# A second edge sort in four steps per block, one more part of edge sums between the experts, and row products in bf16 thirds

## The chip, the core and the metric

The kernel runs on one core of one Trainium2 chip. The metric is the device time of one launch in microseconds; the kernel before takes 3007.59 us, the median of three runs (3007.4 to 3023.45).

## The reference, cut to what matters

Two layers of a graph network over N = 3125 nodes of width 256. The part that this change touches is the feed-forward block of layer 0: a small graph attention over 65536 edges that yields a gate for each node and expert, and four experts, and beside them the sort of the 50000 edges that layer 1 will need.

```python
h = (x_flat @ W_gat).reshape(M, HEADS, NUM_EXPERTS)          # 4 heads x 4
e = leaky_relu(a_src[src] + a_dst[dst], 0.2)
ee = exp(e - segment_max(e, dst)[dst])
alpha = ee / (segment_sum(ee, dst)[dst] + 1e-16)
agg = segment_sum(h[src] * alpha[:, :, None], dst) + b_gat
scores = layernorm(agg).reshape(M, HEADS, NUM_EXPERTS).mean(1)   # top 2, softmax -> gate g
for ei in range(NUM_EXPERTS):
    hh = gelu(x @ W1[ei] + b1[ei])
    out = out + g[..., None] * (hh @ W2[ei] + b2[ei])
# layer 1: the same kind of edge sum over (src, dst), grouped by src
```

## The kernel before, in words

Nodes lie in NT = 25 tiles of P = 125. Edges sorted by their goal node lie in SBUF as columns of 128: COLS0 = 512 columns for this block, COLS1 = 400 for layer 1. The stage is `gat_edges` (L2297). One Block (from L2330) holds everything that follows, and the order on each engine is written out by hand.

**Slots.** `Experts0` (L2689) works through 52 chunks of two node tiles (the last chunk of each expert has one). Each half of a chunk's work is a slot: `tensor_down` of a tile (4 f32 products of 256 columns), or `tensor_up` for the next chunk (4 f32 products of 250 columns). There are 100 downs and 102 ups, so 202 slots, numbered 0 to 201. On TensorE, VectorE and ScalarE the expert work of a slot is followed by `s1....slot(n)` (the second sort) and `by....slot(n)` (rows by products). Slots 38, 118, 163, 197 and 201 are downs, so the line L2787 (`vector_down`, VectorE's part of a down) marks their time.

**The second sort** is `SortBeside` (L1419), 25 blocks of 16 columns. Slots 6 to 30 count. From `rank_at` = 38 each block has USES = 5 slots: `tensor_again` (16 products) and four `tensor_same` (5 products each) share a ring of two PSUM banks, four of the five slots have a `tensor_rank` (12 products). VectorE has `vector_again` and `vector_turned` (one-hot tables), `vector_within` (a scan), `vector_choose` and `vector_base`. So ranks fill slots 38 to 162. At slot 163 VectorE computes all places (`vector_places`) and the first two tables of the moves; from `move_at` = 168 each of 27 blocks moves in two slots (`tensor_half`: 8 products of 400 columns; `vector_move`: four large comparisons and products; `scalar_half`: 4 Signs). The last 20 of these 54 slots, 202 to 221, have no expert work: they are run after the loop, and then `vector_finish` and `tensor_end`.

**Rows by products.** `RowsByProducts` (L1800) makes the last 64 of the 512 columns of gathered rows. In slots 38 to 117, of every five one turns four one-hot tables (`L1874`) and ScalarE copies them to f32 (`L1890`); in each of the other four TensorE multiplies one of them with the node table `m.hg` (20 of its 24 words, 500 columns of f32, L1882), and VectorE picks a row (`vector_take`: L1844 and L1848). The other 448 columns are gathered by GpSimd (L2378).

**Edge sums.** They are made in four parts of columns, PARTS = 0, 128, 256, 400, 512. Parts 0 and 1 start at slots 86 and 150 (PART_AT) and are spread over eleven slots: scores, maxima, Exp on ScalarE, weigh, then two steps of scans. Parts 2 and 3 are run after the sort has ended.

**The end of the Block.** SyncE has one queue. It stores each chunk's outputs (`ex.store`), then waits for VectorE's mark `all_by` after slot 201, loads X back from DRAM (L2360, 3.2 MB), waits for it, loads expert 1's outputs back (L2365, 3.2 MB), waits for the end of the sort (`pre3`), loads experts 2 and 3 back (6.4 MB) and stores parts 2 and 3 of the sums (`keep`, L2333; 256 columns, 3.1 MB). The next Block, `join_nodes` (L2042), begins when the engines have come through this one; its GpSimd gathers (L2085) and part of its VectorE work wait until all four stores of sums have landed (`r_stored` = 64).

Of the kernel before, what the change touches and what calls it, by code (L numbers as in the profile page):

```python
# [1046 lines left out]
class Sort:  # L1047
# [95 lines left out]
    def vector(self, dve):  # L1143
# [22 lines left out]
        self.vector_finish(dve)  # L1166

# [107 lines left out]
    def vector_finish(self, dve):  # L1275
# [22 lines left out]
        dve.tensor_copy(self.rsum[:, :], ed.key[:, cols - 1:cols]).then_inc(self.row3, 1)  # L1298
        dve.wait_ge(self.pre3, 1)
        dve.tensor_scalar(ed.key[:, :], ed.key[:, :], m.ps[2][:, 0:1], -1.0, ALU.add, ALU.add)  # L1300


    def tensor(self, pe):
# [33 lines left out]
        pe.matmul(m.ps[2][:, 0:1], m.low[:, :], self.rsum[:, :], start=True, stop=True).then_inc(self.pre3, 1)  # L1337
# [81 lines left out]
class SortBeside(Sort):  # L1419
# [3 lines left out]
    USES = 5  # L1423

    def __init__(self, m, ed, key_in, other_in, line_in, sb):
# [41 lines left out]
        self.move_at = self.rank_at + self.USES * self.nb + 5  # L1467
        self.slots = self.move_at + 2 * (self.nm + 2)
# [11 lines left out]
    def block_of(self, n):  # L1480

        return divmod(n - self.rank_at, self.USES)

# [26 lines left out]
    def keys_due(self, n):  # L1510

        t, use = self.block_of(n)
        if n == self.FIRST + self.nb + 1:
            return 2
        return t + 3 if use == 0 and 0 <= t < self.nb - 3 else None
# [90 lines left out]
    def vector_slot(self, dve, n):  # L1606
# [7 lines left out]
        elif a == nb + 1:  # L1614
            self.vector_totals(dve)
            self.vector_again(dve, 1)
        elif a == nb + 3:
            self.vector_starts(dve)
            self.vector_turned(dve, 1)
        elif n == self.rank_at - 2:  # L1620
            self.vector_within(dve, 0)
        elif n >= self.rank_at:
            t, use = self.block_of(n)
            if t < nb:
                if use == 2 and t + 1 < nb:
# [5 lines left out]
                elif use == 4 and t + 2 < nb:  # L1631
                    self.vector_again(dve, t + 2)
                elif use == 0 and 1 <= t < nb - 1:
                    self.vector_turned(dve, t + 1)
            elif n == self.rank_at + self.USES * nb:
# [5 lines left out]
            elif n > self.move_at:  # L1641
# [8 lines left out]
    def tensor_slot(self, pe, n):  # L1650
# [14 lines left out]
        elif n >= self.rank_at:  # L1665
            t, use = self.block_of(n)
            if t < nb:
                if use < 2:
                    self.tensor_same(pe, t, use + 2)
                elif t + 1 < nb:  # L1670
                    if use == 2:
                        self.tensor_again(pe, t + 1)
                    else:
                        self.tensor_same(pe, t + 1, use - 3)
                if use < 4:
                    self.tensor_rank(pe, t, use)
            elif n >= self.move_at:
                self.tensor_half(pe, *divmod(n - self.move_at, 2))

# [76 lines left out]
    def tensor_end(self, pe):  # L1756
        pe.wait_ge(self.row3, 1)
        pe.matmul(self.m.ps[2][:, 0:1], self.m.low[:, :], self.rsum[:, :], start=True, stop=True).then_inc(self.pre3, 1)


    def scalar_slot(self, act, n):
# [9 lines left out]
        elif n >= self.rank_at:  # L1771
            t, use = self.block_of(n)
            if t < nb:
                if use < 2:
                    self.scalar_mask(act, t, use + 2)
                elif use > 2 and t + 1 < nb:
                    self.scalar_mask(act, t + 1, use - 3)
            elif n == self.rank_at + self.USES * nb:
# [21 lines left out]
class RowsByProducts:  # L1800
# [4 lines left out]
    def __init__(self, m, ed, G, W, first, saved, place):  # L1805
# [8 lines left out]
        self.turned = [place(f"gp_turned{i}", [128, self.GROUP * 128]) for i in range(2)]  # L1814
# [2408 lines left out]
```

## Time and profile before

| what | value |
| --- | --- |
| median of the runs | 3007.59 us |
| span of the profiled execution, first to last instruction | 3005.8 us |
| the profiled execution's own time | not given beside its span; the runs are 3007.4 to 3023.45 us |
| the chain that ended last | its first piece starts at 2377.12 us |
| TensorE / VectorE / ScalarE / GpSimd busy over the span | 75% / 61% / 45% / 54% |

A stretch row reads: from:to, length, then for each engine its busy us and number of instructions, the granted TensorE clock (1 is full), the mean busy share of the 16 DMA engines and GB/s. A timeline row reads: start, duration, engine, line, operation, out<-in, shape, count, and in brackets the idle time before it and what ended it.

### The profile page before, as it was taken

The numbers are of one execution on the slowest core, as the hardware profiler recorded it, in microseconds if no ns is written. First come the engines' busy times: TensorE is split into PE (matmuls) and PEld (weight loads), VectorE is DVE, ScalarE is ACT, GpSimd is POOL, SyncE is SP. The second block draws the span as 40 slices with busy tenths as digits, with TensorE's granted clock in tenths as the row PEclk, the third lists the DMA queues.
The fourth block names the chain that finished last, engine by engine and source line by source line (L and its number), as shares of the span: only waits on it lengthen the run. The fifth ranks groups of instructions, "written<-read, shape, count | busy, mean of one in ns | idle before, by whom it ended". The sixth has DMA issues, their size and how long they took to land. (4 is left out here: it accounts for less than half of the span.)

```text
span 3005.8 us, 46144 instructions
## 1 busy us (share of the span) xinstructions
PE 2243.0 (75%) x15376; PEld 1792.1 (60%) x15376; DVE 1843.3 (61%) x4040; ACT 1353.1 (45%) x3268; POOL 1630.6 (54%) x1530
## 2 busy tenths in 40 slices
PE   4487393464599999989622678878774499999998
PEld 4362152453577777877321466666663457999997
DVE  7889556799467887577859566666675830111113
ACT  4368334674312232348706237776672121434343
POOL 0246565466487777778541655777773225344441
PEclk9799696777599999999955788888787599999999
DMA  3240033300333223212542535666662132456335
GB/s 85 65 133 1 19 65 66 68 1 1 63 103 73 63 54 92 65 37 49 135 109 57 128 101 192 209 198 200 206 218 91 37 111 69 139 199 212 127 123 133
DMA packets 186604, 307.78 MB, mean 102 GB/s; under 512 B 90556, under 2 KB 142383, under 8 KB 175698
## 3 DMA queue, kind: packets, MB, share of 16 engines
q1 hardware_dynamic: 109312, 174.45, 19.7%
q0 software_dynamic: 77120, 131.25, 16.1%
q8 instruction: 83, 1.36, 0.2%
q14 instruction: 89, 0.73, 0.1%
HBM read 268.76 MB, written 108.92 MB: 126 GB/s over the span
## 5 line engine op out<-in xcount | busy, mean ns | idle before, releaser
L2378 POOL DMA_INDIRECT ge_near<-gat_src,s_other x448 | 493.3, 1101 | 141.2 <-issue 141.2
L3803 POOL DMA_INDIRECT he_buf<-wh_dram,s_other x400 | 390.3, 976 | 163.1 <-issue 118.5
L983 POOL DMA_INDIRECT pl_table<-s_key,s_other x272 | 305.4, 1123 | 248.7 <-DMA pl_table<-s_key,s_other 172.1
L3298 ACT ACTIVATE x_hT<-bank,x_w 128x128 f32<-128x128 f32 x448 | 164.7, 368 | 262.4 <-PE bank L3240 231.3
L3923 ACT ACTIVATE he_buf<-he_buf,he_e 128x128 f32<-128x128 f32 x800 | 236.4, 386 | 2.5
L3240 PEld LDWEIGHTS bank<-x_xT,x_w 128*128 128x128 f32 x1792 | 208.7, 192 | 2.8
L3240 PE MATMUL bank<-x_xT,x_w 128*128 128x128 f32 x1792 | 208.9, 275 | 0.0
L2769 PE MATMUL bank<-arena 128*125 128x256 f32 x800 | 195.7, 388 | 16.5 <-ACT arena L2777 16.2
L3250 PE MATMUL bank<-x_w,x_hT 128*128 128x256 f32 x896 | 202.5, 379 | 0.0
L4035 DVE SCALAR_TENSOR_TENSOR he_buf<-he_buf,he_cont 128x256 f32<-128x256 f32 x375 | 183.0, 488 | 29.2 <-issue 0.4
L2758 PE MATMUL bank<-XT,arena 128*128 128x250 f32 (+1 forms) x832 | 196.3, 380 | 5.4 <-PEq L73 5.4
L2777 ACT ACTIVATE arena<-bank,arena 128x250 f32<-128x250 f32 (+1 forms) x208 | 84.2, 456 | 247.6 <-PE bank L2758 247.5
L2769 PEld LDWEIGHTS bank<-arena 128*125 128x125 f32 x800 | 146.5, 189 | 55.3 <-ACT arena L2777 22.9
L3250 PEld LDWEIGHTS bank<-x_w,x_hT 128*128 128x128 f32 x896 | 166.0, 190 | 20.3
L2758 PEld LDWEIGHTS bank<-XT,arena 128*128 128x128 f32 x832 | 155.2, 196 | 36.8 <-issue 21.1
L2961 POOL DMA_INDIRECT x_w<-in_L_ffn_fall,x_rows x56 | 55.4, 989 | 151.3 <-DVEq L3044 141.6
L2956 POOL DMA_INDIRECT x_w<-in_L_ffn_rise,x_rows x56 | 56.7, 1012 | 136.5 <-ACT x_hT L3298 85.5
L1796 ACT ACTIVATE arena<-row,arena 128x400 f16<-128x400 f16 x216 | 115.9, 615 | 25.3 <-PE bank L1748 17.7
L3042 DVE TENSOR_TENSOR x_ys<-bank,x_w 128x256 f32<-128x256 f32 x56 | 23.8, 424 | 166.0 <-PE bank L3250 166.0
L3030 DVE TENSOR_SCALAR x_goal<-x_xs 128x1 int32<-128x1 f32 x56 | 8.6, 153 | 189.9 <-PE bank L3230 189.9
L1408 ACT ACTIVATE s_far<-bank 128x512 bf16<-128x512 f32 x128 | 76.5, 597 | 89.9 <-PE bank L1359 76.8
L1789 ACT ACTIVATE arena<-bank 128x512 f16<-128x512 f32 x100 | 59.7, 597 | 114.1 <-PE bank L1716 114.0
(785 smaller groups left out, 6008.1 us busy)
## 6 DMA issues: line engine op xcount, KB each, us to landing
he_result<-he_buf SPq DMA_DIRECT2D x25, 2080.0 KB, 7.9
XN<-s_a_dram SPq DMA_DIRECT2D x57, 512.0 KB
x_y<-arena SPq DMA_DIRECT2D x48, 224.0 KB
x_x<-zero SPq DMA_DIRECT2D x1, 7196.0 KB, 42.4
x_xs<-x_x SPq DMA_DIRECT2D x56, 128.5 KB, 2.1
ge_near<-gat_src,s_other POOLq DMA_INDIRECT x448
he_buf<-wh_dram,s_other POOLq DMA_INDIRECT x400, 2.8
arena<-x_y SPq DMA_DIRECT2D x2, 2800.0 KB
```

Source lines behind the costliest of these rows:

```text
L983: pool.indirect_dma_start(out=self.table, out_offset=bass.IndirectOffsetOnAxis(ap=self.goal[:, c:c + 1], axis=0), in_=self.val[:, c:c + 1] ...
L1796: last = act.activation(self.far[:, 4 * h + c, :], self.m.row16[:, 0:self.cols], ACT.Sign, bias=bias[:, at_:at_ + 1])
L2378: pool.indirect_dma_start(out=G[:, c, 0:HF + H], out_offset=None, in_=m.gat_src, in_offset=bass.IndirectOffsetOnAxis(ap=ed.other[:, c:c + ...
L2758: last = pe.matmul(m.ps[2 + i][:, f % 2 * self.CT * P:f % 2 * self.CT * P + n], w.w1[e % 2][:, k, f * 128:(f + 1) * 128], m.XT[:, lo:lo + ...
L2769: last = pe.matmul(m.ps[4 + t % 2][:P, 0:D], self.hT[:, q % 2 * FC + f, j * P:(j + 1) * P], w.w2[e % 2][:, f, :], start=f == 0, stop=f == ...
L2777: last = act.activation(self.hT[:, q % 2 * self.FC + f, 0:n], self.m.ps[2 + i][:, f % 2 * self.CT * P:f % 2 * self.CT * P + n], ACT.Gelu, ...
L3240: done = pe.matmul(m.ps[f % 4][:, 0:TS], self.rw1[b][:, k, f * 128:(f + 1) * 128], self.xT[j][:, k, :], start=k == 0, stop=k == K2 - 1)
L3250: done = pe.matmul(m.ps[4 + j][:, 0:D], self.hT[j][:, f, :], self.rw2[b][:, f, :], start=f == 0, stop=f == FC - 1)
L3298: act.activation(self.hT[u % 2][:, f, :], m.ps[f % 4][:, 0:TS], ACT.Gelu, bias=self.rb1[u % self.B][:, f:f + 1]).then_inc(self.racted, 1)
L3803: pool.indirect_dma_start(out=buf[j][:, c, 0:HF + H], out_offset=None, in_=m.wh_dram, in_offset=bass.IndirectOffsetOnAxis(ap=ed.other[:, t ...
L3923: done = act.activation(f, f, ACT.Copy, scale=e[j][:, c, h:h + 1])
L4035: dve.scalar_tensor_tensor(v[:, c, 0:HF], v[:, c - 1, 0:HF], spread.cont[:, lo + c:lo + c + 1], v[:, c, 0:HF], ALU.mult, ALU.add)
```

## The change

It is made in three places.

1. The sort's blocks get PACE = 4 slots instead of five. The last `tensor_same` of a block moves behind the last `tensor_rank` of the block before, in the same slot; `vector_again` and `vector_turned` come one block later; the load of keys moves from the first slot of a block to the second. The moves now lie in slots 143 to 196, `vector_finish` is in 197, `tensor_end` in 198 and the new `vector_keys` (the last step of finish) in 199. Nothing of the sort is left behind slot 201. The last prefix sum goes to a free column of bank 6.
2. PARTS become four times 128 columns. Part 2 starts at slot 184; only part 3 follows the loop. `keep(2)` moves from the end of SyncE's list to just behind the last `ex.store`, ahead of the wait for `all_by`.
3. The node table is cut into three bf16 parts that add up to it (`vector_thirds`, five operations at slot 37), the turned one-hots are kept in bf16, and each product becomes three bf16 products over 500 columns, added up in the bank.

```diff
 class SortBeside(Sort):
+    PACE = 4
-        self.move_at = self.rank_at + self.USES * self.nb + 5
-        self.slots = self.move_at + 2 * (self.nm + 2)
+        self.move_at = self.rank_at + self.PACE * self.nb + 5
+        self.end_at = self.move_at + 2 * (self.nm + 2)
...
-        return t + 3 if use == 0 and 0 <= t < self.nb - 3 else None
+        return t + 3 if use == 1 and 0 <= t < self.nb - 3 else None
...  (vector_slot)
-                if use == 2 and t + 1 < nb:
+                if use == 0 and t + 1 < nb:
+                    self.vector_again(dve, t + 1)
+                elif use == 1 and t + 1 < nb:
+                    self.vector_turned(dve, t + 1)
+                elif use == 2 and t + 1 < nb:
                     self.vector_within(dve, t + 1)
...
+            elif n == self.end_at:
+                self.vector_finish(dve)
+            elif n == self.end_at + 2:
+                self.vector_keys(dve)
...  (tensor_slot)
-                if use < 4:
-                    self.tensor_rank(pe, t, use)
+                self.tensor_rank(pe, t, use)
+                if use == 3 and t + 1 < nb:
+                    self.tensor_same(pe, t + 1, 1)
...
+            elif n == self.end_at + 1:
+                self.tensor_end(pe)
...  (RowsByProducts)
-        dve.drain()
+        self.vector_thirds(dve)
+    def vector_thirds(self, dve):
+        rest, whole = wide(self.part[0]), self.m.hg[:, :, 0:self.W]
+        for i, third in enumerate(self.thirds):
+            dve.tensor_copy(wide(third), rest if i else whole)
+            dve.drain()
+            if i < 2:
+                dve.tensor_tensor(rest, rest if i else whole, wide(third), ALU.subtract)
+                dve.drain()
...
-            pe.matmul(self.bank[:, 0:NT * self.W].rearrange("p (t w) -> p t w", w=self.W),
-                      self.turned[g % 2][0:P, (kind - 1) * 128:kind * 128], self.m.hg[:, :, 0:self.W],
-                      start=True, stop=True).then_inc(self.made, 1)
+            for i, third in enumerate(self.thirds):
+                last = pe.matmul(self.bank[:, 0:NT * self.W], self.turned[g % 2][0:P, (kind - 1) * 128:kind * 128],
+                                 third[0:P, :], start=i == 0, stop=i == 2)
+            last.then_inc(self.made, 1)
...  (gat_edges)
-            PARTS = ((0, 128), (128, 256), (256, 400), (400, 512))
+            PARTS = ((0, 128), (128, 256), (256, 384), (384, 512))
-            SPREAD_AT, PART_AT = 64, (86, 150)
+            SPREAD_AT, PART_AT = 64, (86, 150, 184)
...  (sync)
+                    keep(2)
                     sp.wait_ge(by.taken, by.n)
                     sp.wait_ge(all_by, 1)
                     x_back.nodes(sp, m.X[:, :], x_kept)
...
-                    keep(2)
                     keep(3)
...  (vector)
                     dve.drain().then_inc(all_by, 1)
-                    for n in range(n, s1.slots):
-                        s1.vector_slot(dve, n)
-                    s1.vector_finish(dve)
-                    scores(2)
-                    maxima(2)
                     scores(3)
-                    weigh(2)
-                    sums(2, range(H))
                     maxima(3)
```

## Rows read from the trace of the kernel before

**Rows 1.** Stretches of the stage: ranks with products, ranks alone, places, moves, join.
```profile
925.90:1207.80 281.90, 267.62 (x2172) 204.69 (x2171) 232.96 (x355) 79.72 (x165) 214.96 (x208) 0.98 0.29 71
1207.80:1323.30 115.50, 113.79 (x1072) 96.46 (x1072) 67.98 (x127) 40.21 (x83) 88.69 (x89) 1.00 0.26 60
1323.30:1343.30 20.00, 11.88 (x47) 9.43 (x46) 14.58 (x26) 6.63 (x14) 15.23 (x14) 0.74 0.17 34
1343.30:1450.20 106.90, 105.72 (x554) 75.44 (x553) 79.46 (x85) 87.27 (x173) 85.88 (x70) 1.00 0.20 43
...
1534.70:1574.00 39.30, 15.39 (x70) 14.78 (x70) 14.21 (x64) 0.63 (x1) 30.33 (x25) 0.50 0.11 9
```

**Rows 2.** Timeline of VectorE: the downs of slots 38, 118, 163 and 197.
```profile
925.89 0.41 DVE L2787 TENSOR_TENSOR arena<-bank,arena 125x256 f32<-125x256 f32 x1
...
1207.81 0.41 DVE L2787 TENSOR_TENSOR arena<-bank,arena 125x256 f32<-125x256 f32 x1
...
1323.29 0.42 DVE L2787 TENSOR_TENSOR arena<-bank,arena 125x256 f32<-125x256 f32 x1 [1.83 <-PE bank L2769]
...
1433.05 0.42 DVE L2787 TENSOR_TENSOR arena<-bank,arena 125x256 f32<-125x256 f32 x1 [0.72 <-PE bank L2769]
```

**Rows 3.** The last stretches: DMA share and GB/s between 1468.0 and 1534.7 us.
```profile
1468.00:1480.20 12.20, 9.52 (x55) 4.91 (x54) 12.05 (x13) 12.20 (x25) 7.02 (x7) 1.00 1.12 265
1480.20:1493.00 12.80, 5.37 (x28) 2.50 (x25) 6.91 (x14) 6.41 (x11) 0.00 (x0) 0.93 0.05 5
1493.00:1534.70 41.70, 3.06 (x12) 2.71 (x12) 35.82 (x82) 2.30 (x4) 0.45 (x2) 0.50 0.89 229
```

**Rows 4.** Timeline of GpSimd: the first gather of the join.
```profile
1534.72 1.23 POOL L2085 DMA_INDIRECT ge_near<-ge_result,gj_end_i  x1 [4.05 <-DMA ge_result<-ge_near]
```

**Rows 5.** Timeline of TensorE around one product and one up.
```profile
1000.40 0.38 PE L1711 MATMUL bank<-neg,ident 128*128 128x512 f16 x1
1000.62 0.39 PE L1716 MATMUL bank<-XN 128*128 128x128 f16 x4
...
1001.29 1.08 PE L1882 MATMUL bank<-hg,X 125*128 125x500 f32 x2
1002.21 1.85 PE L2758 MATMUL bank<-XT,arena 128*128 128x250 f32 x8
1003.90 0.38 PE L1711 MATMUL bank<-neg,ident 128*128 128x512 f16 x1
```

**Rows 6.** Timeline of VectorE: one block of the sort and its takes.
```profile
1017.37 1.20 DVE L1595 TENSOR_TENSOR_SCAN arena<-XN,bank 128x512 f16<-128x512 f16 x1
1018.70 0.68 DVE L1844 TENSOR_TENSOR X<-bank,X 128x500 f32<-128x500 f32 x1
...
1020.51 0.67 DVE L1600 TENSOR_TENSOR arena<-bank,arena 128x512 f32<-128x512 f32 x1
...
1022.87 0.68 DVE L1844 TENSOR_TENSOR X<-bank,X 128x500 f32<-128x500 f32 x1
...
1024.98 1.23 DVE L1537 TENSOR_TENSOR XN<-arena,row 128x2048 f16<-128x2048 f16 x1
...
1026.45 0.68 DVE L1844 TENSOR_TENSOR X<-bank,X 128x500 f32<-128x500 f32 x1
...
1028.26 0.72 DVE L1558 TENSOR_SCALAR XN<-XN,line 128x2048 f16<-128x2048 bf16 x1
```

**Rows 7.** Timeline of VectorE: two choices (L1600) with part 0 between them.
```profile
1106.62 0.68 DVE L1600 TENSOR_TENSOR arena<-bank,arena 128x512 f32<-128x512 f32 x1
...
1131.21 0.69 DVE L1600 TENSOR_TENSOR arena<-bank,arena 128x512 f32<-128x512 f32 x1
```

**Rows 8.** Timeline of VectorE: finish, start of part 2, start of maxima(3).
```profile
1486.61 0.16 DVE L1280 COPY arena<-bank 128x1 f32<-128x1 f32 x1 [4.71 <-PE bank L1752]
...
1492.61 0.75 DVE L2397 TENSOR_TENSOR ge_ke<-ge_near,ge_ke 128x576 f32<-128x576 f32 x1
...
1513.20 1.52 DVE L2406 TENSOR_TENSOR_SCAN ge_near<-ge_pen,ge_near,ge_ke 128x112 f32<-128x112 f32 x4
```

More of the change, by code:

```diff
@@ L1336, in tensor @@
         pe.wait_ge(self.row3, 1)
-        pe.matmul(m.ps[2][:, 0:1], m.low[:, :], self.rsum[:, :], start=True, stop=True).then_inc(self.pre3, 1)
+        pe.matmul(m.ps[6][:, 511:512], m.low[:, :], self.rsum[:, :], start=True, stop=True).then_inc(self.pre3, 1)
     def tensor_count(self, pe, t, j):
@@ L1630, in vector_slot @@
                         self.vector_base(dve, t + 2)
[L1631 to L1635, printed above, removed]
+            elif n == self.rank_at + self.PACE * nb:
                 twice = lambda x: x.unsqueeze(2).broadcast_to((128, self.cols, 2))
@@ L1757, in tensor_end @@
         pe.wait_ge(self.row3, 1)
-        pe.matmul(self.m.ps[2][:, 0:1], self.m.low[:, :], self.rsum[:, :], start=True, stop=True).then_inc(self.pre3, 1)
+        pe.matmul(self.m.ps[6][:, 511:512], self.m.low[:, :], self.rsum[:, :], start=True, stop=True).then_inc(self.pre3, 1)
     def scalar_slot(self, act, n):
@@ L1776, in scalar_slot @@
                 elif use > 2 and t + 1 < nb:
[L1777 to L1778 removed]
+                    self.scalar_mask(act, t + 1, 0)
+                    self.scalar_mask(act, t + 1, 1)
+            elif n == self.rank_at + self.PACE * nb:
                 act.wait_ge(self.negated, 1)
@@ L1813, in __init__ @@
         self.low = [place(f"gp_low{i}", [128, BC, NT + 1], FP16) for i in range(2)]
-        self.turned = [place(f"gp_turned{i}", [128, self.GROUP * 128]) for i in range(2)]
+        self.turned = [place(f"gp_turned{i}", [128, self.GROUP * 128], BF16) for i in range(2)]
         self.part = [place(f"gp_part{i}", [128, NT * W]) for i in range(2)]
+        self.thirds = [place(f"gp_third{i}", [128, NT * W], BF16) for i in range(3)]
         self.bank = m.ps[6]
@@ L2443, in between @@
                             dve.drain()
-                        for q in range(2):
+                        for q in range(len(PART_AT)):
                             if n == PART_AT[q]:
@@ L2504, in _ @@
                                 n += 1
-                    for n in range(n, s1.slots):
-                        s1.tensor_slot(pe, n)
                     pe.wait_ge(ex.kept, ex.E * NT)
-                    s1.tensor_end(pe)
                 @block.scalar
@@ L2519, in between @@
                     def between(act, n):
-                        for q in range(2):
+                        for q in range(len(PART_AT)):
                             if n == PART_AT[q] + 4:
@@ L2538, in _ @@
                                 n += 1
-                    for n in range(n, s1.slots):
-                        s1.scalar_slot(act, n)
-                    weights(2)
                     weights(3)
```

19 lines of the change are left out of this document (11 added, 8 removed).

## The prediction, made before the changed kernel was run

> **What bounds the kernel now.** I read the chain of waits first: it lies wholly in the last stage, behind a barrier, and does not reach the stage of the change. That stage is followed by barriers, so a microsecond that its end moves is a microsecond of the kernel. The stretches of the stage came next. While ranks run beside products (slots 38 to 117) TensorE is busy 267.6 of 281.9 us, VectorE 233.0. With ranks alone (slots 118 to 162) it is 113.8 of 115.5, in the moves 105.7 of 106.9 [rows 1]. So up to 1450.2 us, where VectorE signals `all_by`, TensorE bounds, VectorE is second where products run, and GpSimd (215.0 of 281.9) has room.
>
> From 1450.2 to 1534.7 us another thing bounds. The reader is to see that VectorE looks critical there (finish and then parts 2 and 3 without a pause), and that the DMA engines are critical too. After X, expert 1 comes back until 1480.2 at 265 GB/s. Then there are 12.8 us at 5 GB/s, in which SyncE waits for the end of the sort. Then come 41.7 us at 229 GB/s, 9.5 MB: experts 2 and 3 (6.4 MB) and the two stores of sums (3.1 MB) [rows 3]. The join's first gather starts at 1534.72, released by the last store [rows 4], and 25 gathers later, at about 1574, the join goes on; GpSimd is busy 30.3 of those 39.3 us with it [rows 1]. The end of the stage is therefore: end of slot 201 (E), plus the time until four stores have landed (84.5 us now), plus the join.
>
> **The tail behind E.** The change takes out 20 half moves, the finish, and part 2, which on VectorE last until 1513.2 [rows 8]. For VectorE alone that is a large gain. But the DMA bytes behind E are the same as before: `keep(2)` moves up, yet only behind the last `ex.store`, which waits for the down of slot 201, so it is issued at E and lies ahead of X. The queue then holds 1.6 + 3.2 + 9.6 + 1.6 = 16 MB, as today. Only the 12.8 us pause goes, since `pre3` is long set. What is left is 84.5 - 12.8 = 71.7 us. VectorE's part 3 needs half of what parts 2 and 3 took, about 18 us [rows 8], so `keep(3)` is issued at E + 20 and lies behind experts 2 and 3; its 50 us of cover are the reason that part 2's removal is worth nothing here. Bounds for the rest: 16 MB at 265 GB/s plus 3 us for the wait for X is 63 us, at 229 it is 73 us [rows 3]. I take 71.7, since the rate with several transfers queued is the row at 229. Gain: 13 us (11 to 21).
>
> **What E gains or loses.** Five terms.
>
> *Ranks beside products, 80 slots in both.* They now hold 20 blocks and not 16. A `same` and a `rank` take 0.89 us of TensorE (1000.40 to 1001.29) [rows 5], `again` about 0.46, by 16 products of the kind of which a rank has 12 in 0.45; a block is 4.0, four more are +16. A product takes 0.92 us now (1001.29 to 1002.21), and 512 columns of 16 bit take 0.22 (1000.40 to 1000.62) [rows 5], so three of 500 take 0.65; 64 x 0.27 is -17. TensorE: -1 us. The bounds for three bf16 products: 0.63 if weight loads hide, 0.92 if each shows its load (0 gain, +17).
>
> *VectorE in that stretch.* A block's steps there are 1.3 (scan) + 2.4 (choose, base) + 1.5 (again) + 0.7 (turned) = 5.9 us [rows 6]; four more blocks make 233 + 23.5 = 256.5 us busy of some 281, 91% where it was 83%. TensorE waits for `taken` before each product, so VectorE's lag comes back to it. Its free time per block falls from 3 us to about 1. Part 0, some 16 us of VectorE put into eleven slots, already stretched the time between two choices to 24.6 us [rows 7], where TensorE's own work for a block is 5 x 1.69 + 4.0 + 4 x 0.92 = 16.1 [rows 5]; with a third of the free time the same chunk costs about 4 us more, the spread of slot 64 about 1, and the ordinary blocks 0.15 each, 3 in all. I take +8; bounds 0 (all absorbed) and +24 (VectorE's whole addition).
>
> *Thirds at slot 37.* Five operations of 500 elements at about 0.6 us each with their drains (a take's product over 500 elements is 0.68 [rows 6]), ahead of the first one-hots that TensorE waits for: +3 (2 to 4).
>
> *Ranks alone.* 45 slots in 115.5 us become 20. That takes away 25 expert halves of 1.69 (1002.21 to 1003.90) [rows 5] and four blocks of 4.0: -42 - 16 = -58. The places of slot 163 stall as before, 20 us [rows 1].
>
> *Moves.* Before, 34 move slots lie in the loop, at (1433.05 - 1343.3) / 29 = 3.10 us each [rows 1, 2]. Now there are 54: 167 us, for 107 that the stretch took with all 34. Behind them slots 197 to 201 still have expert work: 4 x 1.7 and the last down's 0.4, and about 4 because the down of slot 199 and the last prefix sum stand behind `vector_finish`, which runs from 1486.61 to 1492.61 today [rows 8]: +11. Part 1 (slot 150) ran beside ranks alone, where VectorE was busy 68 of 115 us; now it falls among moves, where it is busy 79 of 107 [rows 1]. By 16 us against a free 1.5 us in two slots and tables made some 4.5 us ahead, part 1 costs about 4 us, its Exp with two table loads included. Part 2 ends beside the start tables and costs about 1. Bounds for both: 0 and 16. Sum: 167 + 11 + 5 - 107 = +76.
>
> Total for E: -1 + 8 + 3 - 58 + 76 = +28, say +30 with the second choice (of slot 137) standing directly before the places. A check from the other side: TensorE gets 20 x (3.10 - 1.69) = +28 for the moves taken into the loop, -17 for products, and the rest is stalls (+3, +8, +4, +5), +31.
>
> **Sum.** +30 - 13 = +17 us. The profiled execution spans 3005.8 us and the median of the runs is 3007.6, so 1.8 us lie around it: 3007.6 + 17 = 3024.6.
>
> **A rule against the change.** The row that bears on it is the pause of 12.8 us with work behind it at a steady 229 GB/s [rows 3]: the engines took what was queued without a gap. The Trainium skill, DMA: Bandwidth & Descriptors, section Queues, rings and completion order, says that on each DMA engine the descriptors of one ring are consumed in ring order. By that rule `keep(3)`, issued by the same engine behind the reloads, cannot pass them; no row here shows a late small store behind large loads. Without the rule the case is the first rival.
>
> **The rivals.**
>
> *Stores pass the reloads (faster).* If `keep(3)` lands some 7 us after it is issued, whatever is queued, the join starts at E + 27 and not E + 72. Then the sum is +30 - 57 = -27: 2980. For it speaks that VectorE, not the queue, could be read as the bound of the tail; against it that the store issued at about 1529 landed only when 9.5 MB had been moved at an even rate. No row shows the order itself.
>
> *VectorE keeps up (no change).* All lag is absorbed: E = -1 + 0 + 3 - 58 + 71 = +15 to +18, less 13: about +4, 3012. For it: the free 1 us per block; against it rows 7, where 3 us were not enough.
>
> *VectorE bounds the ranks (slower, far).* Place: slots 38 to 117, the wait of each product for `taken`. Price: its whole 24 us, and among the moves 10, while TensorE's pauses let the granted clock fall as in the stretch of the places (0.74 [rows 1]). It decides once the work of a block on VectorE, dead time included, passes the 13.6 us of TensorE's. E = +47, sum +34: 3042.
>
> That the change does not do what it says could be where GpSimd's gathers (to 1477 today) end after E and hold part 3; by the 50 us of cover it would cost nothing.
>
> **How the numbers follow.** Forecast 0.52 (own range 3012 to 3036), stores pass 0.12, VectorE keeps up 0.22, VectorE bounds 0.14. A measurement of this kernel tells 0.5% (15 us) from no change. The forecast's own spread lies on both sides of that line, 0.31 beyond it; with the third rival slower is 0.45. Within: 0.21 and the second rival, 0.43. Faster 0.12. The range 2998 to 3042 leaves out most of the first rival and the far side of the third.
>
> **What would show it.** E at about 1480 (the last down's end). Three L1882 products per column, 0.65 us apart in all. The time between two choices about 13.6 to 14 us with products and 11 without; move slots still 3.1. After E: no stretch below 100 GB/s until the first L2085, about 72 us later; VectorE idle for some 40 us before the join's L2126. The prediction is wrong in its tail if L2085 starts well before E + 63, in its stalls if E is below 1470 or above 1495.

## The result, and the profile after

The changed kernel takes 3017.38 us (median of 20 runs, 3005.58 to 3024.82), the kernel before in the same session 3008.09 us (20 runs, 3000.18 to 3023.45): a ratio of 1.0029 (95% interval 1.0020 to 1.0038), some 9 us slower. 3024.6 was forecast. The profiled execution spans 3019.1 us, for 3005.8 before.

The stage after, by the same marks as [rows 1, 3]: slots 38 to 117, ranks alone (slots 118 to 137), the places, the moves to the end of slot 201, the tail to the join's first gather, the gathers. The columns are the stretch, its length, busy us and instructions of PE, PEld, DVE, ACT and POOL, the granted clock, the DMA share and GB/s.

```profile
931.40:1215.00 283.60, 266.79 (x2571) 214.93 (x2571) 253.67 (x393) 89.84 (x181) 216.03 (x212) 0.98 0.30 78
1215.00:1268.70 53.70, 53.22 (x537) 45.43 (x536) 26.26 (x47) 17.45 (x37) 41.74 (x40) 1.00 0.24 53
1268.70:1286.00 17.30, 11.90 (x49) 9.36 (x48) 14.37 (x26) 6.51 (x14) 13.41 (x13) 0.80 0.14 23
1286.00:1471.30 185.30, 174.41 (x899) 126.86 (x896) 151.68 (x206) 141.84 (x275) 147.66 (x117) 0.99 0.16 36
1471.30:1543.70 72.40, 3.05 (x12) 2.70 (x12) 23.43 (x64) 1.78 (x3) 14.59 (x17) 0.52 0.90 224
1543.70:1583.00 39.30, 15.38 (x70) 14.77 (x70) 10.13 (x49) 0.00 (x0) 30.32 (x25) 0.50 0.09 8
```

E is now 1471.3 us, for 1450.2: 21.1 later, of which 2.4 stood between the two kernels before slot 38's work began (slot 36's down is 919.5 us before and 921.9 after), in code that is the same in both. The change's own share is 18.7, of the forecast's 28 to 30. The tail fell from 84.5 to 72.4 us (forecast 71.7), the 12.8 us at 5 GB/s of [rows 3] are gone, and the gathers again take 39.3. So the first gather of the join is 9.0 us later (1543.73, for 1534.72 in [rows 4]), of which the change's share is 18.7 - 12.1 = 6.6. The two spans differ by 13.3 us: the other 4.3 lie behind that gather (1471.1 us before, 1475.4 after), in stages that the change does not touch.

| | before | after | difference | forecast |
|---|---|---|---|---|
| slots 36 to 38 (the thirds) | 6.4 | 9.5 | +3.1 | +3 |
| slots 38 to 118 | 281.9 | 283.6 | +1.7 | +7 |
| ranks alone | 115.5 | 53.7 | -61.8 | -58 |
| from the last rank slot to E | 126.9 | 202.6 | +75.7 | +76 |
| E to the join's first gather | 84.5 | 72.4 | -12.1 | -13 |
| sum | | | +6.6 | +15 (said: +17) |

What ends the tail (the time from E, the end of slot 201, to the join's first gather) is told by the waits of three engines. These lines of the timeline after are VectorE's and GpSimd's:

```profile
1489.04 0.94 POOL L2403 DMA_INDIRECT ge_near<-gat_src,s_other  x1 [0.30 <-issue]
1496.90 0.69 DVE L2422 TENSOR_TENSOR ge_ke<-ge_near,ge_ke 128x512 f32<-128x512 f32 x1 [25.64 <-DMA ge_near<-gat_src,s_other]
1542.87 7.36 DVE L2151 TENSOR_SCALAR ge_near<-gj_node,gj_less,gj_final 128x125 f32<-128x125 f32 x25 [17.75 <-DMA ge_result<-ge_near]
1543.73 1.35 POOL L2110 DMA_INDIRECT ge_near<-ge_result,gj_end_i  x1 [26.18 <-DMA ge_result<-ge_near]
```

and these are SyncE's (here L2361 is a store of sums, `X<-x_kept` the load of X, and `arena<-x_y` x4 and `XN<-x_y` are the reloads of experts 1, 2 and 3):

```profile
1472.09 0.35 SPq L2361 DMA_DIRECT2D ge_result<-ge_near  x1
1472.55 1.36 SPq L115 DMA_DIRECT2D X<-x_kept  x2
1494.68 1.73 SPq L115 DMA_DIRECT2D arena<-x_y  x4
1496.45 0.79 SPq L115 DMA_DIRECT2D XN<-x_y  x2
1515.54 0.34 SPq L2361 DMA_DIRECT2D ge_result<-ge_near  x1
```

The reader is to see two things. Part 3 did not start behind the end of the moves: VectorE sat idle for 25.64 us until GpSimd's last gathers had landed, E + 25.6. And the last store was issued at 1515.54 and awaited until 1543.7, 28.2 us, with the reloads ahead of it. The forecast had put the issue at E + 20 and given it 50 us of cover; it was E + 44, so the cover was 28 us, of which the store's own bytes take some 7 (7.5 us in E9). It was still enough, and the tail came out as forecast. E7 shows how near it was to being too little.

### The profile page after: what moved, and what is told of

Same layout as the page of the kernel before. It is cut to its first block and busy times, and to the rows that moved or that the text cites. A ratio compares the mean times of both kernels' runs of the same rounds, so it can differ in the third digit from the quotient of the medians.

```text
span 3019.1 us, 46283 instructions
## 1 busy us (share of the span) xinstructions
PE 2222.3 (74%) x15440; PEld 1788.0 (59%) x15440; DVE 1841.1 (61%) x4045; ACT 1356.9 (45%) x3270; POOL 1640.4 (54%) x1530
## 3 DMA queue, kind: packets, MB, share of 16 engines
q0 software_dynamic: 77120, 131.25, 15.5%
## 5 line engine op out<-in xcount | busy, mean ns | idle before, releaser
L2403 POOL DMA_INDIRECT ge_near<-gat_src,s_other x448 | 499.8, 1116 | 142.1 <-issue 142.1
L2782 PE MATMUL bank<-arena 128*125 128x256 f32 x800 | 198.1, 391 | 17.1 <-ACT arena L2790 17.1
L1412 ACT ACTIVATE s_far<-bank 128x512 bf16<-128x512 f32 x128 | 76.4, 597 | 90.2 <-PE bank L1363 77.1
```

The lines of the kernel that those rows point to most:

```text
L2403: pool.indirect_dma_start(out=G[:, c, 0:HF + H], out_offset=None, in_=m.gat_src, in_offset=bass.IndirectOffsetOnAxis(ap=ed.other[:, c:c + ...
L2782: last = pe.matmul(m.ps[4 + t % 2][:P, 0:D], self.hT[:, q % 2 * FC + f, j * P:(j + 1) * P], w.w2[e % 2][:, f, :], start=f == 0, stop=f == ...
```

## Experiments

The kernels were run in four groups, each beside the kernel before on one chip. In the groups of E1 to E4, of E9 to E11 and of E12 every kernel, the one before too, took some 3675 to 3740 us. Some 570 to 600 us of that are pauses of up to 133.6 us each between slots 8 and 22 of the stage (see the last section), and some 110 to 135 us lie in later stages (from the join's first gather to the end it is 1583 to 1608 us, for 1471 to 1475). From slot 38 to the join's gathers these profiles agree with the others (slots 38 to 201: 539.6 us in E1, 539.5 in the changed kernel), so of them the ratios and these stretches are used, not the times. One thing differs and matters for the tail: here GpSimd's gathers of rows have all been issued before slot 22's down, while without the pauses the last one is issued behind E (1489.04). What E1 to E4 and E9 to E12 say of the tail is therefore said for gathers that are not late. "Tail" is from here on the time from the last down of slot 201 to the join's first gather: 90.2 us in the kernel before (1444.5 to 1534.7), 72.9 after (1470.8 to 1543.7).

**E1: x_early.** The changed kernel, with X loaded behind chunk 44.

```
                             keep(1)
+                            sp.wait_ge(by.taken, by.n)
+                            x_back.nodes(sp, m.X[:, :], x_kept)
...
-                    sp.wait_ge(by.taken, by.n)
                     sp.wait_ge(all_by, 1)
-                    x_back.nodes(sp, m.X[:, :], x_kept)
```

> The changed kernel, but X is loaded back after the store of part 1 (chunk 44), and no longer behind slot 201. Theory (after the loop the queue's bytes bound): 3.2 MB and one wait for a landing leave the tail, so the time from the end of slot 201 (E) to the join's first gather falls from 72.4 us to 55 to 58, E stays at its place within 2 us, and the kernel gains 14 to 17 us on the changed one: about 3001. Rival (VectorE's part 3 or GpSimd's gathers bound the tail): the first gather stays at E + 72, no gain.

Tail 55.6 us (2058.7 to 2114.3), 17.3 less than after. The ratio to before is 0.9990 (0.9977 to 1.0003), by which it is some 12 us of 3008 faster than the changed kernel at 1.0029, in another session. SyncE's stores of sums, and GpSimd's first gather:

```profile
2059.89 0.34 SPq L2361 DMA_DIRECT2D ge_result<-ge_near  x1
2062.78 2.14 SPq L115 DMA_DIRECT2D arena<-x_y  x4
2064.97 0.79 SPq L115 DMA_DIRECT2D XN<-x_y  x2
2077.92 0.34 SPq L2361 DMA_DIRECT2D ge_result<-ge_near  x1
```
```profile
2114.25 1.34 POOL L2110 DMA_INDIRECT ge_near<-ge_result,gj_end_i  x1 [34.32 <-DMA ge_result<-ge_near]
```

The store was issued 19.3 us behind the last down, near the forecast's 20 (here no gather of sums was late), and 36.3 us passed until the join's gather. In that time the stretches show:

```profile
2059.20:2078.00 18.80, 0.00 (x0) 0.00 (x0) 16.97 (x35) 1.15 (x2) 0.00 (x0) 0.57 1.01 270
2078.00:2114.20 36.20, 3.06 (x12) 2.71 (x12) 6.44 (x30) 0.63 (x1) 0.45 (x2) 0.50 0.88 216
```

216 GB/s for 36.2 us are 7.8 MB: the rest of the reloads of experts 2 and 3 (6.4 MB) and the store itself (1.6). Where no gather is late, what binds the tail after the change is the queue, and the 3.2 MB of X that left it are the 17.3 us, with SyncE's wait for X.

**E2: before_x_early.** The same edit in the kernel before.

> The same edit in the kernel before. Theory: there expert 1 then comes back 17 us sooner, but the next transfers wait for the end of the sort at 1492.6 us whatever came before, so the pause of 12.8 us only becomes about 30 and the join's first gather stays at E + 84: no gain, 0 to 1 us. Rival (the tail was bound by its bytes in the kernel before as well): a gain of 14 to 17 us, 2992.

Ratio 0.9998 (0.9975 to 1.0021). The tail is 90.2 us (2045.0 to 2135.2), to the tenth that of the kernel before. Its stretches, from the reload of expert 1 on:

```profile
2051.00:2061.50 10.50, 7.76 (x43) 3.51 (x41) 10.28 (x10) 10.50 (x22) 0.00 (x0) 1.00 1.01 278
2061.50:2098.60 37.10, 20.01 (x106) 9.50 (x104) 30.43 (x41) 25.58 (x48) 0.00 (x0) 0.90 0.20 47
2098.60:2135.20 36.60, 3.06 (x12) 2.71 (x12) 31.02 (x74) 2.30 (x4) 0.45 (x2) 0.50 0.85 222
```

The bytes that go early come back as a longer pause (37.1 us at 47 GB/s, where 12.8 at 5 stood). Before the change the chain was the 20 half moves, then the reloads; behind the change the pause is not there, and the same edit gives 17.3 us.

**E3: store_first.** The changed kernel with the last store issued between the reloads of experts 2 and 3.

```
                     ex.reload(sp, 2)
-                    ex.reload(sp, 3)
                     keep(3)
+                    ex.reload(sp, 3)
```

> The changed kernel, with the last store of sums issued ahead of the load of expert 3. Theory (stores keep their place in the queue): VectorE has part 3 ready at E + 44, 11.2 MB are moved by then or shortly after, so the store lands at E + 53 to 58 and not 72: a gain of 14 to 19 us, about 3000. Rival (engines serve what is queued side by side, so the place in the list does not matter): first gather at E + 68 to 72, a gain under 4.

Tail 57.4 us (2069.8 to 2127.3), 15.5 less than after; ratio 0.9979 (0.9959 to 0.9999). One expert's reload is 3.2 MB, 14 us at 229 GB/s, and it is this that the store no longer waits for. A place in the list thus costs what stands ahead of it: the order holds. The Trainium skill, DMA: Bandwidth & Descriptors, section Queues, rings and completion order, says that each DMA engine consumes a ring's descriptors in order; E1, E3 and E9 agree: from the issue of the last store to the gather it is 36.3 us behind the reloads of experts 2 and 3, 33.4 behind those of 1 and 2 (issued only just before it, since X was awaited) and 7.5 behind what was left of expert 1's.

**E4: part2_behind.** The changed kernel with all of part 2 put back behind the loop, ahead of part 3.

```
-            SPREAD_AT, PART_AT = 64, (86, 150, 184)
+            SPREAD_AT, PART_AT = 64, (86, 150)
...  (sync)
-                    keep(2)
                     sp.wait_ge(by.taken, by.n)
...
+                    keep(2)
                     keep(3)
...  (vector)
+                    scores(2)
+                    maxima(2)
+                    weigh(2)
+                    sums(2, range(H))
                     scores(3)
```

> The changed kernel, with part 2 of the sums (128 columns) and its store behind the loop again, as before the change; the sort stays in its four-slot order. Theory: the tail's bytes are the same and VectorE has cover there, so the time from E to the first gather stays 72 within 2 us, and E comes 0 to 3 us sooner since part 2 no longer stands among the moves: 0 to 3 us faster than the changed kernel, 3014 to 3018. Rival (VectorE bounds the tail): the 17 us of part 2 come on top, 3034.

Tail 72.3 us (2073.8 to 2146.1), for 72.9 after; ratio 1.0022 (0.9999 to 1.0044). VectorE is busy 49.2 us of the first 96 behind the last down, for 33.5 in E3, and the join starts no later. Part 2's move out of the tail is worth nothing with this queue. E did not come 0 to 3 us sooner, as expected: slots 38 to 201 take 541.1 us, 1.6 more than after.

**E5: f32_products.** The changed kernel with the product by the f32 table, as before: tables copied to f32, one product of 500 columns, no thirds.

```
-            for i, third in enumerate(self.thirds):
-                last = pe.matmul(self.bank[:, 0:NT * self.W], self.turned[g % 2][0:P, (kind - 1) * 128:kind * 128],
-                                 third[0:P, :], start=i == 0, stop=i == 2)
-            last.then_inc(self.made, 1)
+            pe.matmul(self.bank[:, 0:NT * self.W].rearrange("p (t w) -> p t w", w=self.W),
+                      self.turned[g % 2][0:P, (kind - 1) * 128:kind * 128], self.m.hg[:, :, 0:self.W],
+                      start=True, stop=True).then_inc(self.made, 1)
```

> The changed kernel with the products in f32 again (no thirds, one f32 product of 500 columns). Theory A (TensorE still bounds the ordinary blocks beside products, which now take 13.1 us, its own work): 64 x 0.27 us come back, blocks of about 14.0, less where part 0 stretches them anyway; the stretch from slot 38 to 118 grows from 283.6 to 293 to 299, slot 37 saves 3: 7 to 12 us slower than the changed kernel. Theory B (VectorE bounds that stretch, busy 253.7 of 283.6): the stretch grows by under 4 us and slot 37 saves 3: within 1 us of the changed kernel.

3023.44 us for 3009.31 of before, ratio 1.0044 (1.0031 to 1.0056). Slots 38 to 118 take 291.3 us, 7.7 more than after. The two downs:

```profile
923.13 0.41 DVE L2798 TENSOR_TENSOR arena<-bank,arena 125x256 f32<-125x256 f32 x1
1214.45 0.42 DVE L2798 TENSOR_TENSOR arena<-bank,arena 125x256 f32<-125x256 f32 x1
```

The products in parts are worth 7.7 us in this stretch, less than half of the forecast's 17, and between what the two theories expected (9 to 15, and under 4). The times between two choices (L1600 in the kernel before, the step that VectorE does once per block) say where the rest is. An ordinary block takes 13.9 us (mean of 14), for 13.2 after, but the three blocks with part 0 take 17.1, 17.0 and 19.6 in the one and 17.3, 17.3 and 19.6 in the other, the block with the spread 16.9 in both, and the one behind part 0 13.5 and 14.5. Where VectorE sets the pace, a shorter product gives nothing. With the 3.1 us of the thirds taken off, the products in parts are worth 4.6. The two ratios agree (1.0044 and 1.0029: 4.5 us), but they come from two sessions, and their intervals together leave 0 to 9.

**E6: thirds_alone.** The kernel before, with the products in three parts and nothing else of the change.

> The kernel before with nothing but the thirds: products as three bf16 products. Theory: TensorE bounds blocks of five slots (16.9 us, VectorE busy 83%), so each product gives 0.27 us; the stretch from slot 38 to 118 falls from 281.9 by 12 to 17 us, slot 37 costs 3: 9 to 14 us faster than before, about 2996. Rival (the product's time is hidden by the wait for VectorE's take): under 4 us less in the stretch, 0 to 3 us slower than before.

3008.10 us for 3009.31, ratio 0.9990 (0.9973 to 1.0008): no change that can be told. Slots 38 to 118:

```profile
923.88 0.41 DVE L2801 TENSOR_TENSOR arena<-bank,arena 125x256 f32<-125x256 f32 x1
1199.22 0.41 DVE L2801 TENSOR_TENSOR arena<-bank,arena 125x256 f32<-125x256 f32 x1
```

275.3 us, 6.6 less than before, where 12 to 17 were expected, and 3.1 more for the cut at slot 37 (36 to 38: 9.5 us, for 6.4). Ordinary blocks go from 16.8 to 16.2 us for 4 products, 0.16 each and not 0.27. This is the mechanism of the rival, for half of the gain: TensorE's waits for VectorE's take (its product, L1844 before) grow from 13.9 us in this stretch to 22.8, so 8.9 of the 17 us were handed to that wait.

**E7: short_take.** The changed kernel; `vector_take`'s sum over the 25 node tiles is left out (a copy of 20 columns stands in its place), so VectorE has some 0.9 us less per product (the sum takes 1.10 us, the copy 0.18).

```
-        dve.tensor_reduce(self.G[:, self.lo + c, 0:W], part.rearrange("p (t w) -> p w t", w=W), AX.X, ALU.add)
+        dve.tensor_copy(self.G[:, self.lo + c, 0:W], part[:, 0:W])
```

> The changed kernel, with the sum over 25 node tiles in each take left out: a copy of 20 words stands in its place, so 64 columns of rows are not what they should be. It takes about 0.8 us of VectorE from each of 64 takes, 51 us. Theory (TensorE bounds ordinary blocks, VectorE only those around part 0 and the spread): ordinary blocks stay at 12.9 to 13.3 us, the blocks around part 0 lose most of their 16 us: the stretch from slot 38 to 118 falls from 283.6 to 266 to 272. Rival (VectorE bounds all blocks): blocks fall below 12 us, the stretch to 250 or less.

One execution, 3010.92 us. Slots 38 to 118 take 267.8 us, 15.8 less than after. The choices of the blocks with part 0, of the changed kernel and then of this one:

```profile
1088.87 0.69 DVE L1605 TENSOR_TENSOR arena<-bank,arena 128x512 f32<-128x512 f32 x1
1106.21 0.68 DVE L1605 TENSOR_TENSOR arena<-bank,arena 128x512 f32<-128x512 f32 x1
1123.52 0.68 DVE L1605 TENSOR_TENSOR arena<-bank,arena 128x512 f32<-128x512 f32 x1
```
```profile
1074.74 0.69 DVE L1605 TENSOR_TENSOR arena<-bank,arena 128x512 f32<-128x512 f32 x1 [0.45 <-PE bank L1742]
1089.20 0.68 DVE L1605 TENSOR_TENSOR arena<-bank,arena 128x512 f32<-128x512 f32 x1
1103.24 0.68 DVE L1605 TENSOR_TENSOR arena<-bank,arena 128x512 f32<-128x512 f32 x1
```

17.3 us apart there, 14.5 and 14.0 here. Over the spread and part 0 the blocks took 16.9, 17.3, 17.3, 19.6 and 14.5 us and now take 14.5, 14.5, 14.0, 17.2 and 12.7: 12.7 of the 15.8 us. The ordinary blocks go from 13.2 to 13.0. So VectorE's lag sits in five blocks, and the others are TensorE's.

The tail of this run is a second result, and it limits what can be said of the tail elsewhere. The last down is at 1446.5 us, 24.3 earlier than the changed kernel's, but the join's first gather is at 1536.87, only 6.9 earlier: the tail is 90.4 us, for 72.9. Its lines:

```profile
1469.34 1.85 SPq L115 DMA_DIRECT2D arena<-x_y  x4
1482.57 0.94 POOL L2403 DMA_INDIRECT ge_near<-gat_src,s_other  x1 [0.30 <-issue]
1511.37 0.69 DVE L2422 TENSOR_TENSOR ge_ke<-ge_near,ge_ke 128x512 f32<-128x512 f32 x1 [64.44 <-DMA ge_near<-gat_src,s_other]
1530.00 0.34 SPq L2361 DMA_DIRECT2D ge_result<-ge_near  x1
1471.00:1511.30 40.30, 0.00 (x0) 0.00 (x0) 0.00 (x0) 0.00 (x0) 9.46 (x11) 0.50 1.00 229
```

VectorE waited for the gathered rows until 28.8 us behind the issue of the last gather; in the changed kernel that was 7.9 us (1489.04 to 1496.90). In those 40.3 us the three reloads moved at 229 GB/s. From 1470 to 1490 us the gathers' own DMA queue moved 172 packets, where it moved 425 in 20 us before E of the changed kernel (1450 to 1470). In the changed kernel 279 packets of gathers got through from 1490.0 to 1494.6, while SyncE waited for X and had nothing else queued. Here the reloads began before the last gathers were issued. So in this one execution the gathers got through slowly beside large loads, and those that had not landed when the reloads began held part 3 until these ended. The store and the join then wait for VectorE and GpSimd, not for the queue: the last store needed 6.9 us (1530.00 to 1536.87).

**E8: part1_early.** The changed kernel with part 1 at slot 126, beside ranks alone, in place of 150.

```
-            SPREAD_AT, PART_AT = 64, (86, 150, 184)
+            SPREAD_AT, PART_AT = 64, (86, 126, 184)
```

> The changed kernel with part 1 of the sums at slot 126 instead of 150, that is beside ranks alone and not among the moves. Theory: VectorE is busy 26 of 54 us there, so part 1 costs nothing, and the 5 to 6 us by which slots 148 to 169 exceed 3.10 each go: E and the kernel 4 to 6 us sooner. Rival (the slots lose that time to something other than VectorE's lag, such as the chunk of places just before): under 2 us.

3021.18 us, ratio 1.0028 (1.0018 to 1.0039): nothing won, where slots 38 to 201 were expected 4 to 6 us shorter. They take 542.2 us, for 539.5. Slots 150 to 169 get shorter, 65.2 to 61.4, so part 1 cost 3.8 us there; but the last blocks of the ranks go from 11.1, 11.1 and 10.2 us to 13.2, 14.3 and 12.7:

```profile
1229.87 0.69 DVE L1605 TENSOR_TENSOR arena<-bank,arena 128x512 f32<-128x512 f32 x1 [1.87 <-PE bank L1742]
1243.07 0.69 DVE L1605 TENSOR_TENSOR arena<-bank,arena 128x512 f32<-128x512 f32 x1
1257.38 0.69 DVE L1605 TENSOR_TENSOR arena<-bank,arena 128x512 f32<-128x512 f32 x1
1270.06 0.69 DVE L1605 TENSOR_TENSOR arena<-bank,arena 128x512 f32<-128x512 f32 x1
```

VectorE is busy 26.3 of 53.7 us in that stretch, and 16 us put into it in pieces still cost 7.8: a mean of free time does not say that a chunk fits between a scan that TensorE waits for and the next.

**E9: after_tail.** E1's edit, and the last store behind the reload of expert 1.

```
                     ex.reload(sp, 1)
+                    keep(3)
                     sp.wait_ge(s1.pre3, 1)
                     ex.reload(sp, 2)
                     ex.reload(sp, 3)
-                    keep(3)
```

> The changed kernel with two edits to SyncE's list behind the loop: X comes back from chunk 44 on (not behind the end of slot 201), and the last store of sums is issued behind the reload of expert 1, ahead of the reloads of experts 2 and 3. Theory A (one queue in order; the small store waits for all that stands before it): in the changed kernel the last store is issued 44.7 us behind the last down (1470.8 to 1515.5) and lands at 72.9; it then needs only its own time, some 5 to 8 us, so the join's first gather starts 50 to 54 us behind the last down and the kernel takes about 2996 us (2990 to 3002), since the 28 us of reloads 2 and 3 then run beside the join. Theory B (the reloads bind what follows the join, or slow the join's gathers): the first gather comes as early, but the join and what follows lose what was won, and the kernel stays at 3010 us or above.

Ratio 0.9916 (0.9886 to 0.9946), faster than before by some 31 of 3734 us (20 to 43 by the interval). The tail is 26.8 us (2063.7 to 2090.5), 63.4 less than the kernel before's, and slots 36 to 201 take 23.7 us more, so some 40 were to be had:

```profile
2064.20:2083.00 18.80, 0.00 (x0) 0.00 (x0) 16.96 (x35) 1.15 (x2) 0.00 (x0) 0.57 0.95 262
2083.00:2090.50 7.50, 1.34 (x5) 1.28 (x6) 1.73 (x10) 0.00 (x0) 0.48 (x3) 0.50 0.98 320
2090.50:2127.00 36.50, 17.11 (x79) 16.20 (x77) 15.27 (x66) 0.63 (x1) 29.17 (x25) 0.50 0.88 161
```
```profile
2082.92 0.34 SPq L2361 DMA_DIRECT2D ge_result<-ge_near  x1
2083.30 1.40 SPq L115 DMA_DIRECT2D arena<-x_y  x2
```

The store takes 7.5 us to the gather. The reloads then move at 161 GB/s beside the join's 25 gathers, which take 36.5 us, as in E1 (36.4). Theory B falls: nothing is given back, and the last product with the gates (L3514) comes 114.0 us behind the join's first gather in this run as in the changed kernel. The tail is shorter than the 50 to 54 us expected, since here the gathers were not late. On a chip without the pauses the 26.8 us would not be reached: the last gather is issued 18 us behind E, part 3 takes 18.6 and the store 7.5, so the tail would be 44 us at the least. This is an estimate from the changed kernel's profile and this one; no run shows it. For E1's edit alone, by the same reckoning and E7, the reloads would start at once and hold the last gathers until they end (4 + 42 + 18.6 + 7.5 = 72 us), and nothing would be gained: an estimate too.

**E10: before_tail.** The same two edits in the kernel before.

> The same two edits to SyncE's list in the kernel before: X from chunk 44 on, the last two stores of sums ahead of the reloads of experts 2 and 3. Theory A (there VectorE's parts 2 and 3 end 79 us behind E, and the stores landed 5.7 us later, behind reloads that were then nearly done): the first gather stays at 82 to 86 us behind E and the time is 3004 to 3012 us, no change. Rival (the queue alone was the bound of the tail before, and the parts were hidden): the gather comes 15 to 30 us sooner and the kernel takes 2980 to 2995 us.

Ratio 1.0001 (0.9976 to 1.0027), tail 91.0 us (2043.3 to 2134.3). The last two stores are issued at 2112 to 2128:

```profile
2111.96 15.94 SPq L2336 DMA_DIRECT2D ge_result<-ge_near  x2
2134.28 1.23 POOL L2085 DMA_INDIRECT ge_near<-ge_result,gj_end_i  x1 [1.36 <-DVEq L2104]
```

In the kernel before, VectorE's list (20 half moves, finish, parts 2 and 3) ended the tail as much as the queue did. Opening the queue alone gives nothing (E10), taking VectorE's work out alone gives 17 (90.2 to 72.9, counted from the last down); both together give 63 (90.2 to 26.8), where no gather is late.

**E11 and E12: five_blocks, five_again.** E9, and 80 columns by products (slots 38 to 137, 16 fewer gathers), and the thirds cut at slot 32.

```
-    BLOCKS, GROUP = 4, 4
+    BLOCKS, GROUP = 5, 4
...
-        if n == self.first - 1:
+        if n == self.first - 6:
             dve.wait_ge(self.saved.sem, self.saved.all)
+            self.vector_thirds(dve)
+        elif n == self.first - 1:
```

> The changed kernel with the two edits of SyncE's list, 80 columns by products in place of 64 (slots 38 to 137, so 16 fewer gathers by GpSimd), and the cut of the node table into three parts at slot 32 in place of slot 37. Theory A (part 3 of the sums waits for GpSimd's gathers, which end 19 us behind E): 16 gathers fewer end about 20 us sooner, so part 3 follows part 2 at once, its store is issued some 22 us behind the last down, and the first gather of the join starts at about 28 to 32. TensorE gets 16 times 0.65 us more and VectorE 16 takes more in slots 118 to 137, so that stretch takes 64 to 68 us for 53.7, and the cut costs 0 to 1 for 3: E is 8 to 12 us later than in the changed kernel. Together 2974 to 2986 us. Theory B (the gathers are not what part 3 waits for): the first gather of the join starts no sooner than 48 us behind the last down, and the kernel takes 3000 to 3010 us.

Ratio 0.9838 (0.9800 to 0.9877). Slots 118 to 138 take 64.0 us, for 53.7, slots 38 to 201 549.6, for 539.2 in E9: +10.4 for 16 more products, as expected. Slots 36 to 38 take 6.4 us, so the thirds at slot 32 cost nothing between these two; slots 22 to 36 take 34.3 us, for 33.5 in E9. The tail is 26.6 us, that of E9: with no gather late, fewer of them give nothing here. That this profile is nevertheless ahead of E9's comes from before slot 38 (22.0 us at its down), from the pauses: they last as long as GpSimd's gathers do, and these are 16 fewer. GpSimd's gathers in E9 and here (line, tiles, count, ns least, median and most, first and last start):

```profile
L2403 POOL DMA_INDIRECT ge_near<-gat_src,s_other x448: 938/944/1994, 846.1 to 1447.5; - x150
```
```profile
L2405 POOL DMA_INDIRECT ge_near<-gat_src,s_other x432: 941/947/1882, 844.2 to 1422.3; - x144
```

The last one starts 25.2 us earlier.

> The same kernel as five_blocks, run once more. There every kernel, that before too, took some 3730 us, with four pauses of 134 us near the stage's start in which GpSimd's gathers ran ahead, so that they were never late at the stage's end. If this run is free of these pauses (before near 3008 us): theory A (part 3 waits for the gathers, and 16 fewer end some 20 us sooner) says a first gather of the join 26 to 34 us behind the last down, slots 38 to 201 in 548 to 552 us for 539.4 in the changed kernel, and 2974 to 2986 us in all; theory B (the gathers end late in spite of it) says a first gather at 45 us or more and 2990 to 3000 us. If the pauses are there again, the ratio is 0.980 to 0.988, as there.

The pauses were there again, and the ratio is 0.9885 (0.9826 to 0.9943); the tail 26.4 us (2060.2 to 2086.6). Slots 38 to 201 take 546.4. E11's interval (to 0.9877) ends just below E9's (from 0.9886), E12's covers nearly all of it, and part of what E11 is ahead comes from the pauses, so that 16 columns more are better than none is not shown. What 16 fewer gathers bring on a chip without the pauses, where the last of them land 25.6 us behind E, stays open.

## Why the prediction was right, and where its terms were off

- **The tail** (forecast -13, measured -12.1). Right in size and in mechanism. Same bytes, same order, the pause gone; the rate was 224 GB/s over the whole tail. E1, E3 and E9 show, where no gather is late, that the order of SyncE's list is what places the last store, and E4 that part 2's removal is worth nothing. What was wrong is what stood behind "50 us of cover": gathers that end after E do hold part 3, for 25.6 us, and that left 28 us of it. That it sufficed is in part luck: the last gathers' packets moved in the few us in which SyncE waited for X. In E7, where the reloads came first, the tail was 17.5 us longer.
- **Stores pass the reloads** fell (E1, E3, E9).
- **The thirds** (+3): +3.1 in the changed kernel and in E6.
- **Ranks beside products** (forecast -1 and +8, measured +1.7 in all). The lag of VectorE was sized nearly right: the blocks with part 0 exceed the ordinary ones by 16.1 us, for 11.5 before, the spread by 3.7, for 2.2: +6, where 4 + 1 + 3 was said; E7 takes 12.7 us of these blocks' time away. TensorE's -1 came as its busy time (266.8 us, for 267.6 [rows 1]), but its idle time rose by only 2.5 us. What was left out is the time that an ordinary block loses beyond TensorE's own work (16.1 us of own work before and 12.8 after): 16.8 us between two choices before, 13.2 after. That is 0.7 x 16 = 11 us of lost time before and 0.4 x 20 = 8 after, some 3 us that no term of the forecast held. The profile names about half of it: the waits for VectorE's take are 0.35 us in an ordinary block before and 0.17 after. E5 splits the stretch in another way: the four-step order costs 9.4 us and the products give 7.7 back, not 17, since in the blocks where VectorE sets the pace they give nothing. The ordinary block's 13.2 us lie below the time that was said, 13.6 to 14.
- **VectorE keeps up** fell in its mechanism: its condition (no lag) is not met, five blocks show it. In numbers it came as close as the forecast or closer: the measured 3017.4 is 5.4 us from its 3012 and 7.2 from 3024.6, and E's 18.7 is next to its +15 to +18, not to +28. The times alone would not have told the two apart.
- **VectorE bounds** fell: 253.7 us busy, as computed (256.5), but the ordinary block stays at TensorE's pace.
- **Ranks alone** (forecast -58, measured -61.8). Between two choices lay 13.1 to 13.6 us in most of these blocks before, and 11.1 now, 2 to 2.5 less a block, while a slot less of expert work is 1.69. The four-slot order also loses less time per block. This and the term above are the 9 us by which E came earlier than forecast.
- **Moves** (forecast +76, measured +75.7). 3.11 us a slot (169 to 185 in 49.8 us), as said; part 1 costs 3.8 (E8), as said (4).
- **The sum.** +6.6 and not +17 in the profile, +9 in the medians. E at 1471.3 lay just inside the 1470 to 1495 that was given, and only with the 2.4 us that are not the change's: by its own sign the forecast's stalls were as good as too large. The direction and the mechanism stand, with half of the size. The step that was mis-sized is the time lost per block outside TensorE's own work, in the two stretches of ranks.

## What to carry to other kernels

Two lists can end a stretch together, an engine's and a queue's; shortening one gives only the difference, and it takes both edits to see the gain (0, 17 and 63 us here, where no gather was late). Then ask what comes third: without the pauses the gathers would, and in E7 they landed late beside the large loads (what ending them sooner would bring, no run here shows). A small store that releases the next stage belongs ahead of large loads that nobody awaits yet. Compare blocks by the time between two marks and not by the bounding engine's own work, since what it loses between slots changes with their number; and price a chunk of work in the intervals it falls into, not by the stretch's mean of free time.

## What the runs showed of the hardware

- GpSimd's gathers mostly took 0.94 to 1.5 us, but two took over 4 at once, while VectorE went through part 2's scans and a move's products:

```profile
1444.27 4.79 POOL L2403 DMA_INDIRECT ge_near<-gat_src,s_other  x1 [0.30 <-issue]
1449.37 4.34 POOL L2403 DMA_INDIRECT ge_near<-gat_src,s_other  x1 [0.30 <-issue]
```

  The same pair stands at the same place in E5 (4.80 and 4.35) and E7 (4.80 and 4.36), the first of it in E8 (4.79); in the kernel before, which has no part 2 there, the longest gather took 3.65. Whether the scans slow them was not tried.
- Where every kernel took some 3730 us, ScalarE waited six times for SyncE's load of the next keys, up to 133.6 us, while GpSimd's gathers went on and 9 GB/s moved (900 to 1400 us of E1). The longest waits of E1 from 800 to 1500 us (engine, tile, line, what it waited for, us in total, times, longest):

```profile
ACT arena L2790 <- DMA XN<-s_a_dram: 485.2, 6, 133.6
DVE XN L1542 <- remote: 441.6, 11, 65.6
```

  It is in every kernel of these groups, the two made from the kernel before too, and in none of E5 to E8. In all eight profiles the down of slot 22 comes 31 to 42 us behind the last gather (E1: 1444.8 and 1475.4; E9: 1447.5 and 1481.5; E11: 1422.3 and 1461.8; E12: 1431.5 and 1473.2), so there, as long as GpSimd gathers, SyncE's small loads and stores hardly get through: 308 packets in those 500 us, beside 11965 of the gathers. In the changed kernel's own profile, the same 448 gathers start from 846.2 to 1489.0 and hold nothing up before E. Why it is so on some chips stays open.
- Beside the join's gathers the reloads moved at 161 GB/s and did not lengthen their issue (25 gathers in 36.4 us, 36.4 without them in E1).
- Beside the three reloads at 229 GB/s the gathers of rows landed late: 28.8 us from the last issue to VectorE's start in E7, 7.9 in the changed kernel.
